# Routing steps of the vector engine moved between the row maxima in the cross-attention stage of a decoder layer

## Chip, cores and metric

One core of a Trainium2 chip. The metric is the device time of one execution in microseconds; three runs of the kernel before gave 829.99, 830.89 and 832.61 us, median 830.89 us.

## The reference

One decoder layer on x of shape (2, 1024, 256), float32, with a context of (2, 77, 192):

```
x = x + self_attention(layernorm(x))       # 16 heads of 16, window of 64 keys
x = x + cross_attention(layernorm(x), ctx) # 16 heads of 64 over 77 context rows
x = x + ffn(layernorm(x))                  # shared FFN and 8 experts, top 2
```

The part that the change touches is the routing of the FFN:

```
logits = xf @ router_w + router_b
routing = softmax(logits)
sel_w, sel_idx = top_k(routing, 2)
combine = zeros(T, 8).at[arange(T)[:, None], sel_idx].add(sel_w / (sum(sel_w) + 1e-9))
for e in range(8):
    residual += combine[:, e:e+1] * (gelu(xf @ exp_w1[e] + exp_b1[e]) @ exp_w2[e] + exp_b2[e])
```

## The kernel before

The 2048 tokens are 16 tiles of 128 rows. The kernel is written by hand, one instruction stream for each engine, with semaphores between them. Its stages follow each other: preparation of the weights, self attention (until some 265 us), cross attention with the routing (268 to 444 us), the first groups of the shared FFN, the experts over blocks of 128 routed rows (from 488 us), and the last groups of the shared FFN with the combination.

The cross-attention stage is a software pipeline. Function `cross(i, par, on)` exists once for each engine, is called for i = 0 to 22, and in iteration i works on several tiles at once: `on[n]` says that the step for tile i - n is in this iteration. The steps of one tile are spread over eight iterations:

- on[0] layer norm: `moments`, `variance` (VectorE, lines 1412, 1417, 1419), the inverse deviation (GpSimd, line 489), `normalized` (line 1424, tile xn2)
- on[1] transpose of xn2 (TensorE, line 927), its high part by ScalarE and the rest by VectorE (xt2h, xt2l)
- on[2] scores of all 16 heads in three PSUM banks (TensorE, `split_product`, three matmuls for each product: lines 265 to 267), `peak(0)`, `peak(1)`, `peak(2)` (VectorE, line 1589: minus the row maximum of the 6, 6 and 4 heads in a bank), and the exponentials head by head (ScalarE, line 1250), bank after bank, each bank waiting for its peak; den is the sum, its reciprocal is line 1654
- on[3] prob times the reciprocal (GpSimd, line 586, 128x1232), transposes of prob (TensorE, line 956), high part (ScalarE)
- on[4] `low(0)`, `low(1)`, `low(2)` (VectorE, line 1351, tile ptl), product with the values (TensorE, lines 265 to 267), added into X (VectorE, line 1647), third layer norm
- on[5] XN3c (VectorE, line 1424), its transposes (TensorE, line 946) and the logits (TensorE, line 965)
- on[6] routing on VectorE: logits plus bias (1598), `dve.max` (1605), `dve.max_index` (1613), `hot` (1624, one-hot rows of the two best experts: iota8 compared with the two indices), `sel` (1629, the sum of the two one-hot rows, bf16), `cum` (1632, running count of the experts, bf16); TensorE makes the rank from sel and cum (972, 973)
- on[7] `slot8` (1594), `prod` (1602, hot times slot), `dest` (1610), and two indirect DMAs that scatter the row (GpSimd, line 611)

GpSimd's own order in an iteration is: normalization of prob (586), a sixteenth of the expert weight split (591 a copy, 593 a subtraction, both SBUF to SBUF, 128x256), shared bias into X (601), inverse deviations (489), indirect DMAs (611).

Every engine runs its instructions in program order. A routing instruction that needs the one before it waits for semaphore `rt` (for sel: `c["sel"]`), which each of them counts up. The tiles hot, iota8, besti, prod, slot8, sel and cum lie in SBUF; the peaks read PSUM. In the function below the change lies between `low(2)` and the update of `cum`.

Of the kernel before, what the change touches and what calls it, by code (L numbers as in the profile page):

```python
# [64 lines left out]
def decoder_layer(nc, x, ctx, wq, wk, wv, wo, last_k, last_v, xq, xk, xv, xo, xb,  # L65
# [612 lines left out]
    def tile_of(t):  # L678
        return X[:, bass.ds(t, 1), :].rearrange("p t d -> p (t d)")
# [668 lines left out]
    def _(dve):  # L1348
        def less_high(o, whole, high):

            return dve.tensor_tensor(o, whole, high.bitcast(F32), ALU.subtract)  # L1351
# [202 lines left out]
        def route(ins):  # L1554

            nonlocal done
            done += 1
            ins.then_inc(rt, 1)
            return done

        def split_group(g):
            dve.wait_ge(h["xh"], g + 1)
            less_high(gxl[:, :, :].rearrange("p c n -> p (c n)"), turned_bank(g), gxh[:, :, :].rearrange("p c n -> p (c n)")).then_inc(h["xl"], 1)

        def group_low(g, pair):
            dve.wait_ge(h["hh"], 4 * g + pair + 1)
            less_high(htl[:, 2 * pair:2 * pair + 2, :].rearrange("p k n -> p (k n)"), up_banks(g)[pair],
                      hth[:, 2 * pair:2 * pair + 2, :].rearrange("p k n -> p (k n)")).then_inc(h["hl"], 1)

        def cross(i, par, on):  # L1570
            def low(k):
                if not on[4]:
                    return
                dve.wait_ge(c["ph"], C + (i - 4) * 3 + k + 1)
                c0, c1 = TCH[k]
                if k < 2:
                    last = less_high(ptl[:, c0:c1, :], cross_t[k].rearrange("p (a n) -> p a n", a=4), pth[:, c0:c1, :])
                else:
                    less_high(ptl[:, c0, :], cross_t[k][:, 0:P], pth[:, c0, :])
                    last = less_high(ptl[0:FLAST, c0 + 1, :], cross_t[k][0:FLAST, P:2 * P], pth[0:FLAST, c0 + 1, :])  # L1580
                last.then_inc(c["pl"], 1)

            def peak(k):
                if not on[2]:
                    return
                ps, h0, h1 = BANKS[k]
                dve.wait_ge(c["exp"], C + (i - 3) * 3 + k + 1)
                dve.wait_ge(c["S"], C + (i - 2) * 3 + k + 1)
                dve.tensor_reduce(negm2[:, h0:h1], ps[:, 0:(h1 - h0) * CK].rearrange("p (h k) -> p h k", k=CK),  # L1589
                                  AX.X, ALU.max, negate=True).then_inc(c["max"], 1)  # L1590

            if on[7]:
                dve.wait_ge(c["rk"], C + i - 6)
                n_slot = route(dve.tensor_tensor(slot8[:, :], rank_ps, base8[:, :], ALU.add))
            if on[6]:
                t = i - 6
                dve.wait_ge(c["lg"], C + t + 1)
                dve.tensor_tensor(logits[:, t, :], cross_l, rb_all[:, :], ALU.add).then_inc(c["lgc"], 1)
            low(0)
            if on[7]:  # L1600
                dve.wait_ge(rt, n_slot)
                n_prod = route(dve.tensor_tensor(prod[:, :, :], hot[:, :, :], slot8[:, :].unsqueeze(1).broadcast_to([P, 2, E]), ALU.mult))
            if on[6]:
                dve.wait_ge(c["lgc"], C + t + 1)
                n_best = route(dve.max(best[:, t, :], logits[:, t, :]))
            low(1)
            if on[7]:
                dve.wait_ge(rt, n_prod)
                with nc.allow_low_precision(reason="slot numbers are whole and small"):
                    dve.tensor_reduce(dest[:, i - 7, :], prod[:, :, :], AX.X, ALU.add).then_inc(c["dst"], 1)  # L1610
            if on[6]:
                dve.wait_ge(rt, n_best)
                n_index = route(dve.max_index(besti[:, :], best[:, t, :], logits[:, t, :]))
            peak(0)
            low(2)
            if i == NT + 2:
                split_group(0)
            if i == NT + 3:
                group_low(0, 0)
                group_low(0, 1)  # L1620
            peak(1)
            if on[6]:
                dve.wait_ge(rt, n_index)
                n_hot = route(dve.tensor_tensor(hot[:, :, :], iota8[:, :].unsqueeze(1).broadcast_to([P, 2, E]),
                                                besti[:, 0:2].unsqueeze(2).broadcast_to([P, 2, E]), ALU.is_equal))
            peak(2)
            if on[6]:
                dve.wait_ge(rt, n_hot)
                dve.tensor_tensor(sel[:, :], hot[:, 0, :], hot[:, 1, :], ALU.add).then_inc(c["sel"], 1)
            if on[6]:  # L1630
                dve.wait_ge(c["sel"], C + t + 1)
                counted = route(dve.tensor_tensor(cum[(t + 1) % 2][:, :], cum[t % 2][:, :], sel[:, :], ALU.add))
                assert t < NT - 1 or counted == RT_COUNTED
            if on[1]:
                dve.wait_ge(c["xh"], C + i)
                less_high(xt2l[:, :, :], cross_x.rearrange("p (c n) -> p c n", c=DC), xt2h[:, :, :]).then_inc(c["xl"], 1)
            if on[5]:
                dve.wait_ge(c["x3c"], C + i - 5)
                normalized3(i - 5).then_inc(c["xn3"], 1)
            if on[0]:  # L1640
                moments(i)
                variance(i)
            if on[4]:
                t = i - 4
                dve.wait_ge(c["o"], C + t + 1)
                xt = tile_of(t)
                dve.tensor_tensor(xt, cross_o, xt, ALU.add).then_inc(c["x2"], 1)
                dve.wait_ge(c["x2"], C + t + 1)
                moments3(t)
                variance3(t)  # L1650
            if on[2]:
                dve.wait_ge(c["exp"], C + (i - 1) * 3)
                dve.wait_ge(c["nrm"], C + i - 2)
                dve.reciprocal(den2[:, 1, :], den2[:, 0, :]).then_inc(c["rd"], 1)
            if on[0]:
                normalized(i).then_inc(c["xn"], 1)
# [7 lines left out]
        for i in range(NT + 7):  # L1664
            cross(i, i % 2, [0 <= i - n < NT for n in range(8)])
            if i == NT + 3:
                group_low(0, 2)
                group_low(0, 3)
                split_group(1)
# [165 lines left out]
```

## Time and profile before

| what | value |
|---|---|
| time of the profiled execution | 830.89 us |
| its span | 829.0 us |
| median of three runs | 830.89 us |
| TensorE matmul busy | 737.9 us (89%), 5593 instructions |
| VectorE busy | 506.9 us (61%), 1185 instructions |
| ScalarE busy | 448.5 us (54%), 1599 instructions |
| GpSimd busy | 388.2 us (47%), 398 instructions |
| mean granted TensorE clock | 0.957 |
| chain that ended last | PE 54%, DVE 13%, issue 11%, ACT 6%, POOL 6%, DMA 1% |

The span is the time from the first to the last instruction of the profiled execution. A busy share is an average over stages with different limits, so the rows below are from one stage. In rows of the profile DVE is VectorE, ACT ScalarE, POOL GpSimd, PE TensorE's matmuls. Recorded instructions of one engine overlap by some 0.08 us when the second waits for nothing.

### The profile page before, as it was taken

The page shows a single profiled execution, that of the slowest core. Times are in us where ns is not written, and L with a number is a line of the kernel's source. Part 1 is how long each engine was busy: PE and PEld are TensorE (multiplying, and loading weights), DVE is VectorE, ACT ScalarE, POOL GpSimd, SP SyncE. Part 2 cuts the span into 40 slices and gives each one's busy share as a digit, 9 for nine tenths or more (in the row PEclk, how much of TensorE's full clock was granted, in tenths as well). Part 3 has the DMA queues.
Part 4 walks back from the last instruction along what each step waited for, and adds up shares of the span by engine and source line. Part 5 has one row for each costly group of instructions (what it writes and reads, how often), then busy time and mean ns, then how long its engine had stood idle before and what let it go on. Part 6 is the DMA issues. An engine that isn't in the chain of part 4 may idle for free.

```text
span 829.0 us, 18311 instructions
## 1 busy us (share of the span) xinstructions
PE 737.9 (89%) x5593; PEld 665.1 (80%) x5593; DVE 506.9 (61%) x1185; ACT 448.5 (54%) x1599; POOL 388.2 (47%) x398
## 2 busy tenths in 40 slices
PE   4998999999984899999988989999999999987198
PEld 4887777778863788999987979999899999986187
DVE  6767778778762577999965455555444545531146
ACT  2548888888872686767853533444333343332052
POOL 4104555555543455777856910799438200007700
PEclk9999999999996899999999999999999999998579
DMA  8415222222130000000322421365515211113411
GB/s 216 133 40 180 88 102 77 75 104 83 70 116 7 1 1 14 26 31 33 127 67 83 153 64 39 121 219 174 172 42 176 68 38 38 45 33 95 119 34 58
DMA packets 47628, 69.65 MB, mean 84 GB/s; under 512 B 4989, under 2 KB 39317, under 8 KB 47573
## 3 DMA queue, kind: packets, MB, share of 16 engines
q1 hardware_dynamic: 37253, 39.58, 14.7%
q0 software_dynamic: 8576, 29.10, 10.6%
q8 instruction: 29, 0.48, 0.2%
q10 hardware_dynamic: 1744, 0.28, 0.2%
q14 instruction: 26, 0.21, 0.1%
HBM read 40.76 MB, written 28.18 MB: 83 GB/s over the span
## 4 chain that ended last, share of the span: by engine, by line
PE 54%; DVE 13%; issue 11%; ACT 6%; POOL 6%; DMA 1%; POOLq 0%; DVEq 0%; ACTq 0%; SPq 0%
PE PQ L265 12%; PE PQ L267 11%; PE PQ L266 11%; PE PQ L1061 4%; ACT prob L1250 3%; POOL prob L507 3%; PE PQ L818 2%; PE PQ L997 2%; PE PQ L999 2%; PE PQ L775 2%; PE PQ L998 2%; DVE ptl L1351 2%; DVE negm L1589 2%; PE PQ L803 2%; POOL prob L513 1%
## 5 line engine op out<-in xcount | busy, mean ns | idle before, releaser
L265 PE MATMUL PQ<-wts,hth 128*128 128x256 f32 x424 | 124.3, 293 | 5.4 <-DVE htl L1351 5.1
L267 PE MATMUL PQ<-wts,htl 128*128 128x256 f32 x424 | 119.7, 282 | 0.0
L266 PE MATMUL PQ<-wts,hth 128*128 128x256 f32 x424 | 119.5, 282 | 0.0
L1351 DVE TENSOR_TENSOR htl<-PQ,hth 128x512 fp32r<-128x512 f32 x106 | 68.8, 686 | 60.9 <-ACT hth L1104 59.9
L1175 ACT ACTIVATE prob<-PQ,negm 128x128 f32<-128x128 f32 x256 | 90.4, 370 | 24.8 <-DVE negm L1461 23.1
L1104 ACT ACTIVATE hth<-PQ 128x512 fp32r<-128x512 f32 x106 | 58.6, 599 | 76.2 <-PE PQ L1061 76.2
L1250 ACT ACTIVATE prob<-PQ,negm 128x77 f32<-128x77 f32 x256 | 79.4, 362 | 35.2 <-DVE negm L1589 35.2
L265 PEld LDWEIGHTS PQ<-wts,hth 128*128 128x128 f32 x424 | 80.8, 190 | 7.9 <-issue 4.8
L1321 ACT ACTIVATE hact<-PQ 128x512 f32<-128x512 f32 x74 | 44.4, 600 | 68.4 <-DVE PQ L1752 63.8
L266 PEld LDWEIGHTS PQ<-wts,hth 128*128 128x128 f32 x424 | 81.2, 192 | 0.0
L267 PEld LDWEIGHTS PQ<-wts,htl 128*128 128x128 f32 x424 | 80.8, 191 | 0.0
L568 POOL TENSOR_TENSOR wts<-raw,wts 128x2048 fp32r<-128x2048 f32 x16 | 73.7, 4609 | 1.4
L1286 ACT ACTIVATE PQ<-PQ,shared_b 128x256 f32<-128x256 f32 x64 | 25.9, 447 | 83.7 <-remote 40.8
L1752 DVE TENSOR_TENSOR PQ<-PQ,b_all 128x512 f32<-128x512 f32 x74 | 51.4, 696 | 29.0 <-PE PQ L267 26.2
L648 POOL DMA_INDIRECT ya<-slots,dest x16 | 15.4, 964 | 103.0 <-DMA slots<-y_sb 98.4
L1747 DVE TENSOR_TENSOR y_sb<-PQ,b_all 128x256 f32<-128x256 f32 x37 | 15.7, 425 | 77.8 <-PE PQ L267 74.7
L265 PE MATMUL PQ<-wts,fxh 128*128 128x512 f32 x148 | 62.0, 419 | 1.1 <-DVE fxl L1351 1.1
L1250 ACT ACTIVATION_READ_ACCUMULATOR prob<-PQ,negm 128x1 f32 x256 | 62.6, 245 | 0.0
L507 POOL TENSOR_TENSOR prob<-prob,rden 128x512 f32<-128x512 f32 x48 | 50.9, 1061 | 17.2 <-DVE rden L1470 16.6
L267 PE MATMUL PQ<-wts,fxl 128*128 128x512 f32 x148 | 58.9, 398 | 0.0
L566 POOL CAST wts<-raw 128x2048 fp32r<-128x2048 f32 x16 | 30.5, 1904 | 60.0 <-PE PQ L267 59.9
L266 PE MATMUL PQ<-wts,fxh 128*128 128x512 f32 x148 | 58.5, 395 | 0.0
(236 smaller groups left out, 2270.0 us busy)
## 6 DMA issues: line engine op xcount, KB each, us to landing
slots<-zeros SPq DMA_DIRECT2D x16, 1024.0 KB, 4.3
raw<-in_L_ffn_exp_w_dram POOLq DMA_DIRECT2D x16, 1024.0 KB, 5.9
xf_sb<-slots SPq DMA_DIRECT2D x39, 128.0 KB, 2.0
slots<-y_sb SPq DMA_DIRECT2D x37, 128.0 KB, 1.7
b_all<-in_L_ffn_exp_b_dram POOLq DMA_DIRECT2D x6, 512.0 KB, 4.2
raw<-in_L_ffn_shared_w_dram SPq DMA_DIRECT2D x2, 1024.0 KB, 6.7
out_dram<-X SPq DMA_DIRECT2D x16, 128.0 KB
X<-in_x_dram SPq DMA_DIRECT2D x1, 1792.0 KB, 23.5
```

The lines of the kernel that those rows point to most:

```text
L265: pe.matmul(o, lh, rh, start=start, stop=False)
L266: pe.matmul(o, lh, rl, start=False, stop=False)
L267: return pe.matmul(o, ll, rh, start=False, stop=stop)
L507: pool.tensor_tensor(prob[s][:, :, :], prob[s][:, :, :], rden[:, q, 4 * s:4 * s + 4].unsqueeze(2).broadcast_to([P, 4, P]), ALU.mult).then_ ...
L568: pool.tensor_tensor(low, raw[:, cols], high.bitcast(F32), ALU.subtract).then_inc(done, 1)
L1061: last = pe.transpose(down_t[:, n, k * P:(k + 1) * P], hact[:, (4 * n + k) * P:(4 * n + k + 1) * P], ident[:, :])
L1104: return nc.scalar.activation(o, i, ACT.Copy, scale=scale)
L1175: last = nc.scalar.activation(prob[s][:, j, :], self_s[:, s % 2, j * P:(j + 1) * P], ACT.Exp, bias=negm[:, q, u:u + 1], accum_out=den[:, q ...
L1250: last = nc.scalar.activation(prob2[par][:, h, :], ps[:, (h - h0) * CK:(h - h0 + 1) * CK], ACT.Exp, bias=negm2[:, h:h + 1], accum_out=den2 ...
L1321: nc.scalar.activation(hact[:, n * 512:(n + 1) * 512], up[:, n, :], ACT.Gelu).then_inc(f["act"], 1)
L1351: return dve.tensor_tensor(o, whole, high.bitcast(F32), ALU.subtract)
L1752: dve.tensor_tensor(up[:, n, :], up[:, n, :], b1_all[:, e % 2, n * 512:(n + 1) * 512], ALU.add).then_inc(f["add"], 1)
```

## The change

In VectorE's `cross`, `hot` is issued ahead of `peak(1)` instead of behind it, and `peak(2)` is issued behind `sel` instead of ahead of it. All instructions, operands and waits stay.

```
             if i == NT + 3:
                 group_low(0, 0)
                 group_low(0, 1)
-            peak(1)
             if on[6]:
                 dve.wait_ge(rt, n_index)
                 n_hot = route(dve.tensor_tensor(hot[:, :, :], iota8[:, :].unsqueeze(1).broadcast_to([P, 2, E]),
                                                 besti[:, 0:2].unsqueeze(2).broadcast_to([P, 2, E]), ALU.is_equal))
-            peak(2)
+            peak(1)
             if on[6]:
                 dve.wait_ge(rt, n_hot)
                 dve.tensor_tensor(sel[:, :], hot[:, 0, :], hot[:, 1, :], ALU.add).then_inc(c["sel"], 1)
+            peak(2)
             if on[6]:
                 dve.wait_ge(c["sel"], C + t + 1)
                 counted = route(dve.tensor_tensor(cum[(t + 1) % 2][:, :], cum[t % 2][:, :], sel[:, :], ALU.add))
```

## Rows read from the trace of the kernel before

**Rows 1.** Timeline of VectorE: start us, duration us, engine, line, operation, tiles, count.
```profile
340.27 0.42 DVE L1647 TENSOR_TENSOR X<-PQ,X 128x256 f32<-128x256 f32 x1
341.63 0.15 DVE L1419 TENSOR_SCALAR stats<-stats 128x1 f32<-128x1 f32 x1
...
344.41 0.47 DVE L1351 TENSOR_TENSOR ptl<-PQ,pth 128x128 fp32r<-128x128 f32 x2
344.80 0.62 DVE L1589 TENSOR_REDUCE negm<-PQ 128x6 f32<-128x462 f32 x1
345.35 1.90 DVE L1624 TENSOR_TENSOR hot<-iota,besti 128x16 f32<-128x16 f32 x1
347.18 0.47 DVE L1589 TENSOR_REDUCE negm<-PQ 128x4 f32<-128x308 f32 x1
347.56 0.15 DVE L1629 TENSOR_TENSOR sel<-hot 128x8 bf16<-128x8 f32 x1
347.75 0.64 DVE L1632 TENSOR_TENSOR cum<-cum,sel 128x8 bf16<-128x8 bf16 x1
348.31 0.41 DVE L1351 TENSOR_TENSOR xt2l<-PQ,xt2h 128x256 fp32r<-128x256 f32 x1
...
349.81 0.41 DVE L1647 TENSOR_TENSOR X<-PQ,X 128x256 f32<-128x256 f32 x1
```

**Rows 2.** Instructions on tile hot: duration ns min/median/max, first and last start us, forms.
```profile
L1624 DVE TENSOR_TENSOR hot<-iota,besti x16: 157/1902/2362, 305.3 to 443.3; 128x16 f32<-128x16 f32 x16
L1629 DVE TENSOR_TENSOR sel<-hot x16: 149/152/168, 306.0 to 443.5; 128x8 bf16<-128x8 f32 x16
L1602 DVE TENSOR_TENSOR prod<-hot,slot x16: 165/166/1762, 311.8 to 444.2; 128x16 f32<-128x16 f32 x16
```

**Rows 3.** Timeline of GpSimd in the same iteration.
```profile
344.95 2.26 POOL L586 TENSOR_TENSOR prob<-prob,den 128x1232 f32<-128x1232 f32 x1
347.14 0.40 POOL L591 CAST wts<-raw 128x256 fp32r<-128x256 f32 x1
347.62 0.74 POOL L593 TENSOR_TENSOR wts<-raw,wts 128x256 fp32r<-128x256 f32 x1
```

**Rows 4.** Timeline of TensorE: first score matmuls of four iterations, x3 transposes.
```profile
332.27 0.46 PE L265 MATMUL PQ<-Ah,xt2h 128*128 x1
...
341.78 0.48 PE L265 MATMUL PQ<-Ah,xt2h 128*128 x1 [0.30 <-issue]
...
349.09 0.20 PEld L946 LDWEIGHTS PQ<-ident,XN3c 128*128 128x128 f32 x2 [0.24 <-DVE XN3c L1424]
...
350.87 0.45 PE L265 MATMUL PQ<-Ah,xt2h 128*128 x1
...
408.06 0.45 PE L265 MATMUL PQ<-Ah,xt2h 128*128 128x462 f32 x1
```

**Rows 5.** Timeline of ScalarE: first exponentials of bank 0 and of bank 1.
```profile
344.52 0.33 ACT L1250 ACTIVATE prob<-PQ,negm 128x77 f32<-128x77 f32 x1 [2.28 <-DVE negm L1589]
...
346.60 0.36 ACT L1250 ACTIVATE prob<-PQ,negm 128x77 f32<-128x77 f32 x1
```

**Rows 6.** Timeline of an iteration in which X waited for TensorE.
```profile
330.74 0.42 DVE L1647 TENSOR_TENSOR X<-PQ,X 128x256 f32<-128x256 f32 x1 [1.30 <-PE PQ L267]
...
335.28 0.62 DVE L1589 TENSOR_REDUCE negm<-PQ 128x6 f32<-128x462 f32 x1
335.42 2.26 POOL L586 TENSOR_TENSOR prob<-prob,den 128x1232 f32<-128x1232 f32 x1
```

**Rows 7.** Timeline of two iterations with a shorter lead, second peak or hot.
```profile
383.00 0.62 DVE L1589 TENSOR_REDUCE negm<-PQ 128x6 f32<-128x462 f32 x1
383.06 2.27 POOL L586 TENSOR_TENSOR prob<-prob,den 128x1232 f32<-128x1232 f32 x1
...
410.91 0.64 DVE L1589 TENSOR_REDUCE negm<-PQ 128x6 f32<-128x462 f32 x1
411.47 2.36 DVE L1624 TENSOR_TENSOR hot<-iota,besti 128x16 f32<-128x16 f32 x1
411.53 2.26 POOL L586 TENSOR_TENSOR prob<-prob,den 128x1232 f32<-128x1232 f32 x1
```

More of the change, by code:

```diff
@@ L1620, in cross @@
                 group_low(0, 1)
-            peak(1)
             if on[6]:
@@ L1625, in cross @@
                                                 besti[:, 0:2].unsqueeze(2).broadcast_to([P, 2, E]), ALU.is_equal))
-            peak(2)
+            peak(1)
             if on[6]:
@@ L1629, in cross @@
                 dve.tensor_tensor(sel[:, :], hot[:, 0, :], hot[:, 1, :], ALU.add).then_inc(c["sel"], 1)
+            peak(2)
             if on[6]:
```

## The prediction

> **What bounds the kernel now.** I read the page first: span 829.0 us in a run of 830.89 us, so 1.9 us lie outside the span, and the run shown is the median of the three. The change touches one function of one engine, the routing steps of VectorE in the cross-attention stage (some 268 to 444 us), so everything is decided by who sets the length of an iteration there. I went through three views.
>
> The timeline of VectorE over one steady iteration [rows 1]. The add into X starts at 340.27 and again at 349.81: one iteration is 9.53 us, and in between VectorE has no idle time at all. Two of its instructions are far too long for what they do: hot (128x16) takes 1.90 us and cum (128x8) 0.64 us. The group of the routing tile over all 16 tiles says what they cost alone: hot at least 157 ns, median 1902 ns, and prod, of the same size, at least 165 ns but once 1762 ns [rows 2].
>
> The timeline of GpSimd beside it [rows 3]. The normalization of prob runs from 344.95 to 347.21 and hot ends at 347.25; the weight split runs from 347.62 to 348.36 and cum ends at 348.39. Both VectorE instructions end 0.03 to 0.04 us after the GpSimd instruction that was under way. All three that are ever caught (hot, prod, cum) are tensor_tensor with both inputs in SBUF. So the stall isn't a semaphore wait: hot is held by GpSimd's instruction, for about 1.9 - 0.08 = 1.8 us, and cum for about 0.5 us.
>
> The timelines of TensorE and ScalarE, for what would bound next [rows 4, 5]. ScalarE sits idle 2.28 us before the exponentials in every iteration, waiting for the first peak. TensorE has almost no slack: the scores start at 341.78 and 350.87, 9.09 us apart, and in these the one gap is the idle 0.24 us before the x3 transposes, which waited for XN3c. Its floor is 9.09 - 0.24 = about 8.9 us. From the first iteration that stalls to the last the scores start at 332.27 and at 408.06, eight periods in 75.79 us, 9.47 us each.
>
> **The change part by part.** Nothing is added or removed. hot moves ahead of peak(1), and peak(2) moves from between hot and sel to between sel and cum. The new order is low(2), hot, peak(1), sel, peak(2), cum. No wait is added, no DMA is moved, and hot's own wait is for max_index, long done (it stood before peak(0)).
>
> 1. hot. It now takes peak(1)'s place: recorded start 344.80, while GpSimd's normalization starts at 344.95 [rows 1, 3]. An instruction that isn't held is over some 0.16 us after its recorded start, so hot would be done at 344.96, just as the other starts. That 0.15 us lead isn't luck: both engines count from the same instruction, the end of the tile's variance at 341.78. GpSimd does its inverse deviation and two indirect DMAs after it, VectorE the two low parts and peak(0). Where TensorE sets the time of X (330.74, idle 1.30 us before it) the lead is the same: 335.28 against 335.42 [rows 6]. In one iteration it is only 0.06 us, 383.00 against 383.06 [rows 7]. What is a lead worth? With 0.06 us of lead hot once lost all the same: start 411.47, normalization at 411.53, duration 2.36 us [rows 7]. There the instruction in front of it ran until 411.55, so it really began behind. At the new place the one in front ends at 344.88, 0.07 us ahead of 344.95. Cost of hot: 0.08 us net if it wins, up to 2.4 us (344.88 to 347.25) if it loses. I take the win, since the lead is more than twice the one that failed.
>
> 2. peak(1) then starts 0.08 us later than now. ScalarE wants it at 346.60 [rows 5], it is done at 345.50. Free.
>
> 3. sel now comes right behind peak(1), at about 345.42, in the middle of the normalization. It reads both halves of hot, two SBUF inputs, the form of the three that get caught; in this trace it never starts inside such a GpSimd instruction, so its price isn't shown. Bounds: 0.08 us if it is never held, 1.8 us if it is, until 347.25. I take the second, by its form. So the stall isn't removed, it is handed from hot to sel, and peak(2) starts at 347.17 as now. ScalarE needs that only behind the six heads of bank 1: 346.60 plus six times the 0.30 us from one head to the next in this timeline, 348.4.
>
> 4. cum. Now it starts at 347.75, behind the split's start at 347.62, and is held. After the change peak(2) stands in front of it instead of sel with its semaphore round trip, so cum starts where sel starts now: 347.56. sel at this place isn't held: 0.15 us, with the split starting 0.06 us behind it [rows 1, 3], and its longest of 16 is 168 ns [rows 2]. cum has the same size. Bounds: 0.08 us net to the present 0.64. I take the free end, on the nearest row. xt2l then starts at 347.65 instead of 348.31: 0.66 us off VectorE's iteration, 9.53 to 8.87.
>
> What is late next is TensorE, at about 8.9, so the two are level. Eight periods of 8.9 make 71.2 us against 75.79: 4.6 us less. In the iteration behind them (411 us) sel takes hot's lost place and saves at most its own 0.2 us, and ScalarE is busy there; in the next (420 us) no peaks are left and the order is as it was; the first iterations with routing (305 to 327 us) wait for TensorE or have no clash. Nothing for these. Should sel never be held, cum would be caught by the normalization instead, until 347.25, and xt2l would start at 347.17: VectorE at 8.4, TensorE still at 8.9, the same 4.6 us. What follows the stage starts by as much earlier. I take 4.5 us: 830.9 - 4.5 = 826.4 us.
>
> A rule of the Trainium skill bears on this. By the rows alone, hot, prod and cum end with GpSimd's instruction. "SBUF — State Buffer", section "Who interferes with whom", says that a VectorE instruction with two SBUF inputs contends with a GpSimd instruction that reads SBUF, that whoever issues first keeps the shared pair for its whole length, and that the other blocks fully. By that rule sel is held as soon as it stands inside the normalization, and the full 1.8 us of hot can't be had by this move; by the same rule hot at its new place holds GpSimd and not the other way round.
>
> **The rivals.**
> - Hot loses the race: slower. For it: the one case in which hot led by only 0.06 us; the lead is small, and I don't know when GpSimd really begins. Against it: 0.07 us of real lead where that case had 0.02 us of lag. Then hot holds peak(1) behind it until 347.25, so peak(1) ends at 347.79, sel is caught by the split until 348.40, peak(2) ends at 348.79, cum at 348.87, and xt2l starts at 348.79: 0.48 us more per iteration than 348.31. ScalarE's bank 1 begins 1.2 us late, which its 2.28 us of idle absorb. Nine times 0.48 is 4.3 us: 835.2. It decides where hot's start comes within about 0.05 us of the normalization's.
> - Cum is caught after all: no change. The stall moves to sel, cum waits for the split until 348.39 as before, xt2l stays at 348.31. For it: hot at 411.47 had the same recorded lead as sel at 347.56 and was held. Against it: eight iterations in which sel, as small as cum, got through. Time 830.9.
> - Part of the gain is lost: some iterations have the short lead of 383.00, or TensorE's clock falls at another place once the stage is shorter. Halfway, 828.5.
>
> **How the numbers follow.** The forecast 0.55, hot loses 0.20, cum caught 0.17, part of the gain 0.08. A measurement here tells a change from none from about 0.3%, 2.5 us. Faster: 0.55 and nearly half of the last, 0.60. Slower 0.21, no change 0.19. The forecast's own range is 824.8 to 828.2. It and the unchanged case hold too little together, so the range reaches to the slow case: 824.5 to 835.4.
>
> **What would show it.** In VectorE's timeline: hot at 0.16 us, sel at about 1.8 us in the steady iterations, cum at 0.16, X to X in 8.9 us with a short wait for TensorE ahead of X, and the XN3c wait of TensorE gone. Step 1 is wrong if hot stays near 2.4 us with peak(1) behind it; step 3 if sel is at 0.15 us and cum at 1.4; step 4 if cum stays at 0.64 with X to X at 9.53. The whole is wrong if X to X is 8.9 and the span doesn't follow.

## The result and the profile after

The changed kernel is slower: median 837.42 us (834.13 to 842.55, 15 runs) against 832.42 us (829.38 to 835.95, 15 runs) of the kernel before on the same chip. The ratio is 1.0063, 95% interval [1.0046, 1.0081], that is 5.2 us on 830.9 with an interval from 3.8 to 6.7. The profiled execution took 834.44 us, span 832.7 us.

VectorE's timeline over one steady iteration of the kernel after; the columns are those of [rows 1], which it answers to.

```profile
340.20 0.41 DVE L1647 TENSOR_TENSOR X<-PQ,X 128x256 f32<-128x256 f32 x1
...
344.81 2.37 DVE L1623 TENSOR_TENSOR hot<-iota,besti 128x16 f32<-128x16 f32 x1
347.10 0.62 DVE L1589 TENSOR_REDUCE negm<-PQ 128x6 f32<-128x462 f32 x1
347.65 0.66 DVE L1628 TENSOR_TENSOR sel<-hot 128x8 bf16<-128x8 f32 x1
348.23 0.47 DVE L1589 TENSOR_REDUCE negm<-PQ 128x4 f32<-128x308 f32 x1
348.62 0.15 DVE L1632 TENSOR_TENSOR cum<-cum,sel 128x8 bf16<-128x8 bf16 x1
348.69 0.41 DVE L1351 TENSOR_TENSOR xt2l<-PQ,xt2h 128x256 fp32r<-128x256 f32 x1
...
350.19 0.41 DVE L1647 TENSOR_TENSOR X<-PQ,X 128x256 f32<-128x256 f32 x1
```

GpSimd's timeline beside it, kernel after; it answers to [rows 3].

```profile
344.87 2.26 POOL L586 TENSOR_TENSOR prob<-prob,den 128x1232 f32<-128x1232 f32 x1
...
347.55 0.73 POOL L593 TENSOR_TENSOR wts<-raw,wts 128x256 fp32r<-128x256 f32 x1
```

Hot starts at 344.81 by the record, 0.06 us ahead of the normalization, and takes 2.37 us: it ends at 347.18, 0.05 us behind it. Sel then falls into the weight split and ends with it (348.31 against 348.28), with peak(2) behind it. X to X is 9.99 us where it was 9.53. The group of tile hot in the kernel after (duration ns min/median/max) says that this is the rule; in [rows 2] sel never went over 168 ns.

```profile
L1623 DVE TENSOR_TENSOR hot<-iota,besti x16: 157/2144/2454, 304.1 to 447.1; 128x16 f32<-128x16 f32 x16
L1628 DVE TENSOR_TENSOR sel<-hot x16: 149/653/662, 305.1 to 447.3; 128x8 bf16<-128x8 f32 x16
```

How far it reaches: VectorE's timeline of the kernel after at the first X of the steady iterations and the X eight periods later, and of the kernel before at that later X.

```profile
330.20 0.42 DVE L1647 TENSOR_TENSOR X<-PQ,X 128x256 f32<-128x256 f32 x1 [1.30 <-PE PQ L267]
...
409.35 0.41 DVE L1647 TENSOR_TENSOR X<-PQ,X 128x256 f32<-128x256 f32 x1
```

```profile
406.14 0.41 DVE L1647 TENSOR_TENSOR X<-PQ,X 128x256 f32<-128x256 f32 x1
```

Eight periods take 79.15 us after and, from 330.74 [rows 6], 75.40 us before: 3.75 us more, 0.47 us each (seven of the eight are 9.99 and 9.53 us, the last 9.21 and 8.68). The granted clock isn't the reason: it is 1.00 in both from 330 to 406 us, and 0.957 before and 0.961 after over the span. The span is 3.7 us longer, so what follows the stage moved with it. The medians lie 5.0 us apart; what is in them beyond 3.7 the two profiled executions don't show. The first add into X, which comes ahead of every routing step, starts anywhere from 290.9 to 296.8 us in the profiled executions of this study, so spans of single executions differ by some microseconds for reasons that lie ahead of the moved instructions.

In the iteration ahead of these, the granted clock falls in both kernels from 1.00 to 0.50, that is from the level of 2.4 to that of 1.2 GHz; in the kernel before it is 0.50 from 323 to 325 us. TensorE had been busy for only 0.9 us from 320 to 322. The period from X to X around it takes 11.90 us before and 11.69 after. It cancels between these two kernels, but not in all of the comparisons below.

### The profile page after: what moved, and what is told of

It is laid out like the page before. It is cut to its first block, busy times and chain, and to the rows that moved or that the text cites. A ratio compares the mean times of both kernels' runs of the same rounds, so it can differ in the third digit from the quotient of the medians.

```text
span 832.7 us, 18311 instructions
## 1 busy us (share of the span) xinstructions
PE 737.1 (89%) x5593; PEld 664.3 (80%) x5593; DVE 511.1 (61%) x1185; ACT 448.8 (54%) x1599; POOL 388.0 (47%) x398
## 4 chain that ended last, share of the span: by engine, by line
PE 52%; DVE 12%; issue 8%; ACT 8%; POOL 6%; another core or an unknown queue 5%; DMA 1%; POOLq 0%; DVEq 0%; ACTq 0%; SPq 0%
PE PQ L265 12%; PE PQ L267 11%; PE PQ L266 11%; PE PQ L1061 4%; ACT prob L1250 3%; POOL prob L507 3%; PE PQ L818 2%; PE PQ L775 2%; DVE ptl L1351 2%; PE PQ L997 2%; PE PQ L999 2%; PE PQ L998 2%; DVE hot L1623 2%; PE PQ L803 1%
## 5 line engine op out<-in xcount | busy, mean ns | idle before, releaser
L489 POOL TENSOR_TENSOR stats<-stats,minus_half 128x1 f32<-128x1 f32 x48 | 26.6, 553 | 68.0 <-DVE stats L1419 61.0
```

## The experiments

The table has, for every kernel, the ratio to the kernel before with its 95% interval, the time from the first to the last of the 16 adds into X in the profiled execution (from the groups of line 1647, or where that line has moved to), and the steady X to X. The last column has the stretches between the first and the last of these adds in which the granted clock of that execution was 0.50 (times in whole us). The kernel before has 140.0 us, 9.53, and 323-325.

The last column matters for the third: e3 has the steady iterations of the kernel before, but no fall of the clock, and takes 10.16 us for the period that takes 11.90 before, so a fall there is worth some 1.7 us. Why some kernels don't have it isn't shown: in e3 TensorE is nearly as idle, busy 1.1 us of the 2 from 321 to 323, and keeps its clock. Nor is it known whether other executions of a kernel agree with its profiled one in this.

| kernel | ratio | first to last X, us | steady X to X, us | clock at 0.50 |
|---|---|---|---|---|
| after | 1.0063 [1.0046, 1.0081] | 144.0 | 9.99 | 323-325 |
| e1 hot right behind peak(0) | 1.0047 [1.0020, 1.0074] | 146.2 | 9.99 | 325-327, 427-430 |
| e2 hot of one-input compares | 1.0064 [1.0037, 1.0091] | 144.7 | 9.99, once 10.36 | 426-428 |
| e3 peak(2) moved alone | 0.9988 [0.9968, 1.0008] | 138.5 | 9.53 to 9.55 | none |
| e4 all ahead of peak(0), one-input | 1.0269 [1.0230, 1.0308] | 162.8 | 11.86 | none |
| e5 normalization waits for hot | 0.9952 [0.9926, 0.9978] | 134.9 | 9.17 | none |
| e6 waits for cum | 0.9929 [0.9904, 0.9955] | 134.5 | 8.84 to 9.37 | 418-420 |
| e7 the same, hot early | 0.9919 [0.9888, 0.9950] | 132.8 | 8.84 to 9.36 | none |
| e8 an event before it | 1.0063 [1.0037, 1.0090] | 144.0 | 9.99 | 324-327 |
| e9 all three much earlier | 1.0023 [0.9991, 1.0055] | 141.2 | 9.02 to 9.77 | 330-333 |
| e10 hot ahead of peak(0) | one run, 854.28 us | 161.6 | 11.33 to 11.80 | 348-351, 372-375 |
| e11 hot moved alone | 1.0018 [0.9987, 1.0048] | 140.7 | 9.73 | none |

The working picture of all these runs is the prediction's: VectorE and GpSimd share a port, and the one that has it holds the other. The expectations name three theories by letters. A: the normalization takes the port at its recorded start or a little ahead of it, so that more lead is enough (in e2 also: only an instruction with two SBUF inputs is held). B: the indirect DMA in front of the normalization holds already. C: the normalization, queued behind that DMA with nothing to wait for, has the port from well ahead of its recorded start. A lead is the time by which an instruction of VectorE starts ahead of the normalization, by the records.

**e1: more lead.**

```
             peak(0)
+            if on[6]:
+                (hot)
             low(2)
```

> The order of the change, except that hot stands right behind peak(0), ahead of low(2): it starts some 0.55 us ahead of GpSimd's normalization instead of 0.06 to 0.15. Theory A (GpSimd's normalization takes the port it shares with VectorE a little ahead of its recorded start, so a lead of 0.15 us is too short and 0.55 is enough): hot takes 0.16 us, the hold passes to sel (some 1.8 us, to 0.04 us behind the end of the normalization), cum starts 0.06 us ahead of the split and takes 0.15 us, X to X falls to 8.9 us, the time is 4 to 5 us below the kernel before. Theory B (the indirect DMA that GpSimd issues ahead of the normalization holds hot already): hot stands inside the second indirect DMA and is held to the end of the normalization, some 2.8 us, X to X stays at 10.0 us and the time is 4 to 5 us above the kernel before.

Median 836.78 us (10 runs). Where the lead is longest, by 0.55 us, hot is held 2.85 us; at 347.46, right ahead of a normalization at 347.52, it is held 2.37 us. Half a microsecond of recorded lead is worth nothing, so it is no race between the two recorded starts. By these numbers theory B could still stand.

**e2: one input.** Hot is made of two comparisons of the logits with the two best values, each with one tensor input.

```
-                n_hot = route(dve.tensor_tensor(hot[:, :, :], iota8[...], besti[...], ALU.is_equal))
+                dve.tensor_scalar(hot[:, 0, :], logits[:, t, :], best[:, t, 0:1], None, ALU.is_equal)
+                n_hot = route(dve.tensor_scalar(hot[:, 1, :], logits[:, t, :], best[:, t, 1:2], None, ALU.is_equal))
```

> The order of the change, hot at its new place, but made of two tensor_scalar compares (the tile's logits against the best and the second best value), each with one SBUF tensor as input. Theory A (the hold comes from the second SBUF input): both take 0.08 to 0.16 us although the normalization starts beside them, the hold passes to sel, and X to X is 8.9 to 9.1 us if cum gets ahead of the split, 9.6 us if it doesn't. Rival (the place or GpSimd's work as such holds whatever reads SBUF there): one of the two is held to the end of the normalization, X to X is 10.0 us or more, and the time is 5 us above the kernel before.

Median 838.17 us (10 runs). VectorE's timeline of this kernel:

```profile
345.79 2.04 DVE L1623 TENSOR_SCALAR hot<-logits,best 128x8 f32<-128x8 f32 x1
347.74 0.42 DVE L1624 TENSOR_SCALAR hot<-logits,best 128x8 f32<-128x8 f32 x1
```

The one-input form is held as well, the first comparison to the end of the normalization, the second into the cast. "Both inputs in SBUF", which I had read from the three that were caught, isn't the only form: a float32 operation with a scalar, from SBUF to SBUF, is held too.

The Trainium skill has this: "SBUF — State Buffer", section "Who interferes with whom", counts `tensor_scalar` from SBUF to SBUF among the operations that can take both port pairs and so contend. This trace agrees: 2.04 us where the fastest of the 16 took 0.22.

**e3 and e11: the halves of the change.** In e3 only peak(2) moves behind sel; in e11 only hot moves ahead of peak(1).

```
 e3:  peak(1), hot, sel, peak(2), cum
 e11: hot, peak(1), peak(2), sel, cum
```

> Half of the change: peak(2) moves behind sel, hot stays behind peak(1). Theory A: hot is held to the end of the normalization as before (1.9 us), sel and peak(2) follow, cum falls into the split and is held to its end, so X to X stays at 9.5 us and the time is that of the kernel before within 1 us. If the copy between the normalization and the split holds too, sel ends 0.04 us behind that copy. Rival (moving peak(2) behind the routing steps costs by itself, through ScalarE's last bank): 0.3 to 0.5 us per iteration, 3 to 4 us above the kernel before.

> The other half of the change: hot moves ahead of peak(1), peak(2) stays ahead of sel. Theory C: hot is held to the end of the normalization (2.4 us) with both peaks behind it; peak(1) and peak(2) follow, sel is caught by the split for some 0.2 us, cum follows free, so xt2l starts 0.4 to 0.5 us later than in the kernel before: X to X 9.9 to 10.0 us, 3 to 5 us above the kernel before, the whole of what the change costs. Rival (the two halves only cost together): within 2 us of the kernel before.

e3: 832.5 us (10 runs), no change to be told. Its 138.5 us from first to last X are 1.5 below before, which is the clock's 1.7 and nothing of the steady iterations. Sel comes earlier and is caught by the cast:

```profile
347.32 0.29 DVE L1628 TENSOR_TENSOR sel<-hot 128x8 bf16<-128x8 f32 x1
```

e11: 836.02 us (10 runs), X to X 9.73. Here the iteration is 0.2 us longer than before: hot is held to the same point, peak(1) now comes behind the hold and costs 0.54 us there, and of the hold by the split only 0.12 us are left, on sel, where cum had 0.5. The expectation had 9.9 to 10.0. The change has 9.99, so its 0.46 us an iteration are 0.20 from hot's move and 0.26 more from peak(2)'s move once hot has moved: then sel, not shielded by peak(2), meets the split (0.66 us) with peak(2) still to come. Neither half alone is told from zero by its ratio; the split of the 0.46 us rests on the steady iterations of the profiled executions, and e11's ratio also has the missing fall of the clock in it, which hides some of what hot's move costs.

**e4: everything ahead of peak(0).** Sel is one comparison with the second best value, hot two comparisons, max_index is dropped, and sel, hot and cum all stand ahead of peak(0). By the race theory this clears GpSimd altogether.

```
+                dve.tensor_scalar(sel[:, :], logits[:, t, :], best[:, t, 1:2], None, ALU.is_ge)
+                (hot as in e2, cum)
             peak(0)
```

> The routing steps all stand ahead of peak(0), where GpSimd issues its indirect DMAs: sel and hot are tensor_scalar compares of the logits with the best two values (one SBUF tensor each, max_index is gone), cum stays as it is and starts over 0.5 us ahead of the normalization; the three peaks follow with nothing between them but low(2). Theory A: no instruction of VectorE is held by GpSimd, VectorE has 7.3 us of work in an iteration, and TensorE sets X to X at 8.9 us: 4 to 5 us below the kernel before. Rival (the holds cover slack that another engine has anyway, say ScalarE behind the peaks): X to X stays above 9.3 us and the time within 2 us of the kernel before.

It is the worst: 856.27 us (4 runs). VectorE's and GpSimd's timelines of this kernel:

```profile
348.78 2.85 DVE L1613 TENSOR_SCALAR sel<-logits,best 128x8 bf16<-128x8 f32 x1
```

```profile
348.34 0.96 POOL L611 DMA_INDIRECT slots<-XN,dest  x1 [0.30 <-issue]
349.32 2.27 POOL L586 TENSOR_TENSOR prob<-prob,den 128x1232 f32<-128x1232 f32 x1
```

Sel begins 0.54 us ahead of the normalization, inside the second indirect DMA, and ends with the normalization, 2.85 us later. Now all three peaks stand behind it and ScalarE has nothing to do meanwhile: X to X 11.86.

So something takes the port more than half a microsecond ahead of the normalization's recorded start: either the indirect DMA in front of it, or the normalization itself, begun early because nothing keeps it back. (It does wait for the reciprocal of den, line 1654, but that is long done.) The next four kernels part these.

**e5: the normalization made to wait for hot.** The kernel after, and one wait more on GpSimd.

```
                 pool.wait_ge(c["rd"], C + i - 2)
+                if on[6]:
+                    pool.wait_ge(rt, 6 * (i - 6) + 3)
```

> The order of the change; one wait is added on GpSimd: the normalization of prob waits until hot of the same iteration is done. Theory C (the normalization, queued behind the second indirect DMA with nothing to wait for, has the port from the time it is handed over, half a microsecond or more ahead of its recorded start): now it can't be handed over early, so hot takes 0.16 us, the normalization starts some 0.1 us later than in the kernel with the change, sel takes the hold (1.8 us), cum starts just ahead of the split and gets through, X to X is 8.9 to 9.1 us and the time 3 to 5 us below the kernel before. Theory B (the second indirect DMA holds): hot is held to the end of that DMA, a few tenths of a microsecond, and X to X is the same 9.0 us, since the normalization follows hot. Rival (the hold has nothing to do with the normalization): hot stays at 2.4 us.

Median 828.96 us (10 runs), faster than before. VectorE's and GpSimd's timelines:

```profile
344.58 0.16 DVE L1625 TENSOR_TENSOR hot<-iota,besti 128x16 f32<-128x16 f32 x1
344.67 0.63 DVE L1591 TENSOR_REDUCE negm<-PQ 128x6 f32<-128x462 f32 x1
345.22 1.95 DVE L1630 TENSOR_TENSOR sel<-hot 128x8 bf16<-128x8 f32 x1
347.09 0.46 DVE L1591 TENSOR_REDUCE negm<-PQ 128x4 f32<-128x308 f32 x1
347.48 0.15 DVE L1634 TENSOR_TENSOR cum<-cum,sel 128x8 bf16<-128x8 bf16 x1
347.55 0.41 DVE L1353 TENSOR_TENSOR xt2l<-PQ,xt2h 128x256 fp32r<-128x256 f32 x1
347.88 0.57 DVE L1426 TENSOR_SCALAR XN3c<-X,stats 128x256 f32<-128x256 f32 x1
```

```profile
344.89 2.25 POOL L588 TENSOR_TENSOR prob<-prob,den 128x1232 f32<-128x1232 f32 x1 [0.19 <-issue]
```

This is the iteration that I had forecast, up to xt2l: hot 0.16, sel held until the normalization ends, cum ahead of the split. The normalization pays 0.19 us of idle for it. Yet X to X is 9.17, not 8.87: with the wait the normalization starts, and ends, later behind hot, so that xt2l comes 2.97 us behind hot's start where I had 2.85, and XN3c is caught by the split, 0.57 for 0.40. That is 0.12 and 0.17 us. Of the 5.1 us less from first to last X, 2.7 lie in the eight periods and 2.0 in the one in which the clock falls before and not here (9.86 us for 11.90).

Two iterations of this kernel at the end of the stage test theory C once more. VectorE's and GpSimd's timelines of the last normalization:

```profile
417.30 0.16 DVE L1625 TENSOR_TENSOR hot<-iota,besti 128x16 f32<-128x16 f32 x1
417.50 0.17 DVE L1630 TENSOR_TENSOR sel<-hot 128x8 bf16<-128x8 f32 x1
```

```profile
417.62 2.25 POOL L588 TENSOR_TENSOR prob<-prob,den 128x1232 f32<-128x1232 f32 x1 [0.30 <-issue]
```

The normalization had waited for hot until just before, and sel, with a lead of only 0.12 us, is free. In the iteration ahead of it hot is done 0.77 us before the normalization at 409.36, so the added wait is over early, and sel is held for 2.61 us with a lead of 0.30.

**e6 and e7: waiting for cum.** In e6 the order is hot, peak(1), sel, cum, peak(2); in e7 hot stands right behind peak(0), sel and cum behind low(2), then the peaks. In both the normalization waits for cum.

```
+                    pool.wait_ge(rt, 6 * (i - 6) + 4)
```

> The order is low(2), hot, peak(1), sel, cum, peak(2), and GpSimd's normalization waits until cum of the same iteration is done. Theory C: none of the three is held, the normalization starts some 0.9 us later than before (345.8 on the scale of the kernel before), TensorE needs it some 1.4 us after it ends, VectorE's work in an iteration is 7.3 to 7.5 us, TensorE bounds at X to X 8.9 us: 4 to 5 us below the kernel before. Rival (the later normalization or the routing steps between the peaks delay ScalarE or TensorE): X to X above 9.3 us, within 2 us of the kernel before.

> As the one before, but hot stands right behind peak(0), and sel and cum right behind low(2), ahead of peak(1): the normalization is released some 0.5 us earlier, peak(1) comes 0.3 us later. Theory C: none held, X to X 8.9 us, the time within 1 us of the one before and 4 to 5 us below the kernel before. Theory B: hot stands inside the second indirect DMA and is held to its end, 0.5 us.

e6: 826.6 us (11 runs); e7: 826.86 us (6 runs). VectorE's and GpSimd's timelines of e7:

```profile
343.71 0.17 DVE L1619 TENSOR_TENSOR hot<-iota,besti 128x16 f32<-128x16 f32 x1
...
344.20 0.16 DVE L1629 TENSOR_TENSOR sel<-hot 128x8 bf16<-128x8 f32 x1
344.39 0.16 DVE L1632 TENSOR_TENSOR cum<-cum,sel 128x8 bf16<-128x8 bf16 x1
...
346.43 0.67 DVE L1426 TENSOR_SCALAR XN3c<-X,stats 128x256 f32<-128x256 f32 x1
...
348.85 0.42 DVE L1649 TENSOR_TENSOR X<-PQ,X 128x256 f32<-128x256 f32 x1 [0.91 <-PE PQ L267]
```

```profile
343.19 0.96 POOL L613 DMA_INDIRECT slots<-XN,dest  x1 [0.30 <-issue]
344.70 2.25 POOL L588 TENSOR_TENSOR prob<-prob,den 128x1232 f32<-128x1232 f32 x1 [0.56 <-issue]
```

Hot runs in the middle of the second indirect DMA, 0.99 us ahead of the normalization, and isn't held; sel and cum aren't either. So the indirect DMA isn't what holds. The hold isn't gone, though: it has moved on to XN3c, which ends 0.15 us behind the normalization and takes 0.67 us in e7 and 1.2 to 1.45 us in e6, where 0.40 is free. That costs nothing here, since TensorE is the bound now, at a mean of 9.0 us: in e7 X waits for it in every one of these iterations (ten times from 321 to 403 us, 7.4 us in all), and from 330.6 to 402.9 us it is busy for 71.5 of 72.3 us in e7 and 71.4 in e6 and waits for no other engine. e7 and e6 are the fastest kernels of the study, with 0.8% [0.5, 1.1] and 0.7% [0.5, 1.0] off the time of before. Of these gains part lies ahead of the steady iterations. Of e7's 7.2 us from first to last X the eight steady periods have 3.1; the period in which the clock falls before has 2.6 (9.32 us for 11.90), by e3 1.7 of them the clock's. And the one prod that is caught for 1.76 us before and after is free in e5 and e7 (longest of 16: 176 ns) and held for at most 0.61 us in e6, as the normalization waits there too.

**e8: an event without a wait.** One increment of a semaphore that nobody waits for, which is all that the helper `pass_waits` does, is put in GpSimd's stream ahead of the normalization.

```
             if on[3]:
+                pass_waits(pool)
                 pool.wait_ge(c["rd"], C + i - 2)
```

> The kernel with the change; on GpSimd a semaphore increment that nobody waits for stands between the last indirect DMA and the normalization. Theory C in its strict form (what counts is that the normalization is handed over while the DMA is still being issued): if the increment has to wait for the DMA's end, the normalization comes later and hot, ahead of it by 0.1 us or more, is free, with X to X at 8.9 to 9.1 us. If the increment passes at once, nothing changes: hot 2.4 us, X to X 10.0 us, 4 to 5 us above the kernel before. I hold the second for likelier.

836.9 us (10 runs), hot 2.31 to 2.45 us in the steady iterations, X to X 9.99: as without it. Not one more instruction in the queue, but a wait that is still open, keeps the port free.

**e9 and e10: how early is early enough.** e9 issues hot, sel and cum ahead of low(1) and peak(0), in the first indirect DMA and just behind it; e10 is the kernel after with hot right behind max_index, in the second.

```
 e9:  max_index, hot, low(0), sel, cum, low(1), peak(0), low(2), peak(1), peak(2)
 e10: max_index, hot, peak(0), low(2), peak(1), sel, peak(2), cum
```

> All instructions of the kernel before and no wait added; VectorE's order is slot, logits, prod, max, dest, max_index, hot, low(0), sel, cum, low(1), peak(0), low(2), peak(1), peak(2), so hot, sel and cum stand 1.3 us and more ahead of the normalization, beside or ahead of the first indirect DMA. Theory C (the normalization has the port only from about the time the second indirect DMA is under way): none of the three is held; peak(0) comes some 0.9 us later, which ScalarE's idle time absorbs; XN3c (one input, but SBUF to SBUF) may be held by the tail of the normalization or the copy behind it; X to X 8.9 to 9.1 us, 3 to 5 us below the kernel before. If the port is taken a microsecond or more ahead, cum is held for 3 us and the time is 10 us or more above the kernel before.

> The order of the change, but hot right behind max_index, ahead of peak(0): its lead over the recorded start of the normalization is about 1.0 us, at the very start of the second indirect DMA. This brackets where the hold begins: it was there at a lead of 0.55 us. If hot takes 0.2 us or less here, the hold begins between 0.55 and 1.0 us ahead; if it takes some 3.3 us, it begins with the hand-over of the second indirect DMA or earlier, and X to X is 10 us or more.

VectorE's and GpSimd's timelines of e9 in a steady iteration:

```profile
341.70 0.16 DVE L1622 TENSOR_TENSOR cum<-cum,sel 128x8 bf16<-128x8 bf16 x1
```

```profile
341.88 0.96 POOL L611 DMA_INDIRECT slots<-XN,dest  x1 [0.30 <-issue]
342.87 2.26 POOL L586 TENSOR_TENSOR prob<-prob,den 128x1232 f32<-128x1232 f32 x1
```

The same of e10, from its one execution:

```profile
360.69 2.93 DVE L1616 TENSOR_TENSOR hot<-iota,besti 128x16 f32<-128x16 f32 x1
```

```profile
360.33 0.96 POOL L611 DMA_INDIRECT slots<-XN,dest  x1 [0.30 <-issue]
361.31 2.26 POOL L586 TENSOR_TENSOR prob<-prob,den 128x1232 f32<-128x1232 f32 x1
```

In e9 cum, 1.17 us ahead of the normalization and just ahead of the second DMA, is free; in e10 hot, 0.62 us ahead and 0.36 us into the second DMA, is held for 2.93 us. e7's hot was 0.52 us into that DMA and free, with the wait behind it. Prod, of the form of hot, comes closer from both sides. In e10 it starts once 0.64 us ahead of a normalization (429.00) and is held for 2.94 us. In e4 it starts once 0.75 us ahead, 0.24 us into the second DMA, and is free; VectorE's and GpSimd's timelines:

```profile
442.67 0.17 DVE L1602 TENSOR_TENSOR prod<-hot,slot 128x16 f32<-128x16 f32 x1
```

```profile
442.43 0.97 POOL L611 DMA_INDIRECT slots<-XN,dest  x1 [0.30 <-issue]
443.42 2.27 POOL L586 TENSOR_TENSOR prob<-prob,den 128x1232 f32<-128x1232 f32 x1
```

So with no open wait an instruction that starts 0.64 us ahead of the normalization's recorded start is held and one that starts 0.75 us ahead isn't: the boundary lies 0.24 to 0.36 us into the DMA in front.

That e9 gains nothing (836.42 us, 12 runs, not told from before, where 3 to 5 us less were expected) has a cause of its own. In its steady iterations it is shorter than before: eight X periods from 338.18 take 74.75 us against 75.40. But in the first iterations with routing there is no indirect DMA yet and the normalization starts right behind GpSimd's inverse deviation. In the first of them hot (1.21 us) and sel (0.63 us), moved forward, drop into the normalization and the split; in the second prod is held for 1.48 us (1.76 before) with all three still behind it and peak(0) behind these. In both, xt2l then waits 0.97 us for ScalarE. These periods are 10.69 and 10.77 us where before has 9.77 and 9.63.

## Why the prediction was wrong

It forecast 826.4 us; by its own bound for telling a change from none, the kernel is slower. Even the range's upper end of 835.4 lies under the median of 837.42, though the runs of before beside it lie 1.5 us above the three that were shown.

- **Step 1, hot: this one failed.** The prediction put the recorded lead of 0.15 us over the recorded starts and took hot to be done as the other starts. In the change hot was held for 2.32 to 2.45 us in the steady iterations, at leads of 0.01 to 0.15 us. What failed is the measure, not just the size of the lead: 0.54 us (e4), 0.55 (e1) and 0.62 (e10) were held too, and 0.31 us (hot) and once 0.12 (sel) were enough in e5, where the normalization had to wait. The hold begins before the record of the instruction that holds. The bound from above, 2.4 us, was right, and the one case with 0.06 us of lead [rows 7] had shown it; I explained it away by the end of the instruction in front.
- **Step 2, peak(1) free.** True only with step 1. Held, it ended at 347.72 and ScalarE's first exponential of bank 1 started at 347.76, against 346.60 [rows 5], after an idle of 1.01 us. That was absorbed, as the rival said.
- **Step 3, sel takes the hold over.** Right where it could be tried: 1.95 us in e5. In the change itself hot took the hold and sel the split's.
- **Step 4, cum slips ahead of the split.** 0.15 us in e5, as forecast. In the change it is free because it comes behind the split.
- **The next bound.** TensorE at about 8.9 us: e7 runs at a mean of 9.0 with X waiting for TensorE each time. But the forecast's order with hot free gives 9.17 (e5), since XN3c is caught by the split, 0.17 us, which I hadn't seen because it stood behind it. And "nothing" for the first iterations was wrong for e5 to e7: they did have a clash, prod's 1.76 us, which went (in e6 it is at most 0.61), and the period of 11.90 us fell to 9.3 to 9.9, by e3 some 1.7 us of it because the clock didn't fall. The last rival had thought of the clock; in the change itself it fell where it had fallen before (11.69).
- **The rival "hot loses the race"** had the chain right, instruction by instruction: sel caught by the split until 348.40 (348.31), xt2l at 348.79 (348.69), 0.48 us more per iteration (0.47). Its 835.2 us is 1.0052 of 830.9, inside the interval of the ratio. It had a chance of 0.20; its condition, hot's start within 0.05 us of the normalization's, was far too narrow.

"SBUF — State Buffer", section "Who interferes with whom", of the Trainium skill says that whoever issues first has the shared pair for its whole length. I read "issues" as the recorded start. The traces agree with the rule only if GpSimd's issue is taken 0.64 us or more ahead of that. "Perfetto Trace Analysis", section "Summary: the profiler window per engine type", of the Trainium skill says that the wait queue and the start of the prefetch are hidden from a VectorE record, and most things from the record of a GpSimd instruction that neither reads nor writes. The normalization does both, so that row doesn't say that its record begins late; e10 shows that something is missing: hot is held over 0.62 us in which no GpSimd instruction but the DMA is recorded.

Shown is that a hold ahead of the normalization's recorded start needs the normalization to have no open wait, that the DMA alone doesn't do it, and that it begins between leads of 0.75 and 0.64 us. That GpSimd's sequencer hands the normalization over while the DMA still runs is an argument from these, not a measurement; nor is the exact moment known.

## What to carry to other kernels

Where an engine shares a port with another, don't take the recorded start for the moment at which it takes the port: here an instruction queued with no open wait behind a DMA of 0.96 us held its rival from up to 0.64 us ahead of its own row. Don't look for a gap in time, make an order: let the long instruction wait for the short ones (0.19 us of idle on GpSimd in e5 and 0.56 in e7 went with kernels 0.5 and 0.8% faster, 2.7 and 3.1 us of it in the eight steady periods). Before you credit an order with all of a gain, look at the granted clock beside the change. And when a stall ends with another engine's instruction and can't be told from busy time, a move only chooses who stands behind it, so count what does.

## What the runs showed of the hardware

- An indirect DMA on GpSimd with no ready tensor instruction behind it didn't hold two-input operations. VectorE's and GpSimd's timelines of the kernel before, at the end of the stage:

```profile
443.31 0.18 DVE L1624 TENSOR_TENSOR hot<-iota,besti 128x16 f32<-128x16 f32 x1
443.53 0.17 DVE L1629 TENSOR_TENSOR sel<-hot 128x8 bf16<-128x8 f32 x1
443.73 0.16 DVE L1632 TENSOR_TENSOR cum<-cum,sel 128x8 bf16<-128x8 bf16 x1
```

```profile
443.15 0.97 POOL L611 DMA_INDIRECT slots<-XN,dest  x1 [0.30 <-issue]
444.43 0.97 POOL L611 DMA_INDIRECT slots<-XN,dest  x1 [0.30 <-issue]
```

  All three run inside the DMA from 443.15 to 444.12 in 0.16 to 0.18 us; what is queued behind it is another DMA. This stood in the trace of before.
- A comparison of 128x8 float32 values took 2.85 us (e4) where 0.22 us is its free time (e2): a factor of 13 by its place alone, with no idle time and no releaser in its row.
- Sel at 347.56 in the kernel before, 0.06 us ahead of the split, was never held in eight iterations. In the program the split waits for the cast in front of it; the normalization has no such wait. This agrees with the rest, but no run takes that wait away.
